# A third bank for the scores of the second attention, taken from the transposes

## The reference, cut to what matters

```python
q = _apply_rope(q, cos, sin)
k = _apply_rope(k, cos, sin)
k = jnp.repeat(k, groups, axis=2)
v = jnp.repeat(v, groups, axis=2)
scores = jnp.einsum('bqhd,bkhd->bhqk', q, k) * scale
scores = jnp.where(causal[None, None], scores, jnp.finfo(scores.dtype).min)
probs = jax.nn.softmax(scores, axis=-1)
attn = jnp.einsum('bhqk,bkhd->bqhd', probs, v).reshape(B, S, NH * HD)
```

## Time and profile before

| | us |
|---|---|
| median of 3 timed runs | 2964.31 (2962.42 to 2965.41) |
| the profiled execution's own time | 2973.27 |
| its span in the profile | 2971.6 |
| second attention: from the first transpose of a stack to the last score | 1585.9 to 2231.6 |
| PE / DVE / ACT / POOL busy over the whole span | 2476.5 / 1614.6 / 1474.1 / 903.1 |

### The profile page before, as it was taken

The page is one execution under the profiler, slowest core; times in us unless marked ns, Lnnn a source line. Parts: engine busy times, 40 slices in busy tenths (PEclk is TensorE's granted clock), DMA queues, the critical chain, the costliest instruction groups (busy, mean ns, idle before and its releaser), DMA issues. The chain is left out here.

```text
span 2971.6 us, 56781 instructions
## 1 busy us (share of the span) xinstructions
PE 2476.5 (83%) x12274; PEld 1400.6 (47%) x12275; DVE 1614.6 (54%) x4317; ACT 1474.1 (50%) x3174; POOL 903.1 (30%) x1721
## 2 busy tenths in 40 slices
PE   4999999999999999998366888898886508999980
PEld 3555565555655566555232333333324504666650
DVE  6666645666366655663586777777743301222227
ACT  3666645666366645563384766667763202222222
POOL 0344433444244434445031222222220171122210
PEclk7999999999999999998786999999989559999995
DMA  2000100001010110111233110111106422111114
GB/s 95 19 23 25 40 23 18 25 26 40 14 26 25 32 31 18 27 26 25 64 159 97 27 29 25 32 31 31 32 16 188 182 101 93 46 46 44 46 41 170
DMA packets 152514, 152.85 MB, mean 51 GB/s; under 512 B 66944, under 2 KB 122240, under 8 KB 150656
## 3 DMA queue, kind: packets, MB, share of 16 engines
q1 hardware_dynamic: 143680, 128.79, 14.3%
q0 software_dynamic: 6528, 17.87, 1.7%
q10 hardware_dynamic: 2112, 4.19, 0.4%
HBM read 87.80 MB, written 47.52 MB: 46 GB/s over the span
## 5 line engine op out<-in xcount | busy, mean ns | idle before, releaser
L1191 ACT ACTIVATE b_P<-b_SC 128x512 f32<-128x512 f32 (+3 forms) x768 | 347.2, 490 | 197.9 <-PE b_SC L1289 184.2
L296 POOL TENSOR_TENSOR a_A<-a_A,a_P 128x512 f32<-128x512 f32 (+3 forms) x320 | 321.4, 1004 | 304.4 <-PE a_O L600 291.8
L448 ACT ACTIVATE a_P<-a_SC 128x512 f32<-128x512 f32 (+3 forms) x640 | 293.4, 469 | 229.8 <-PE a_SC L583 189.8
L506 DVE CUSTOM_DVE_ANT_0 a_MX<-a_MX,a_causal 128x128 f32<-128x128 f32 (+3 forms) x512 | 250.0, 501 | 203.4 <-PE a_MX L649 191.6
L1238 DVE CUSTOM_DVE_ANT_0 b_MX<-b_MX,b_causal 128x128 f32<-128x128 f32 (+3 forms) x512 | 250.9, 500 | 146.4 <-PE b_MX L1333 127.0
L582 PE MATMUL a_SC<-a_QR,a_KR 128*128 128x512 f32 (+3 forms) x768 | 320.3, 421 | 7.0 <-DMA a_QS<-a_minusT 2.9
L649 PE MATMUL a_MX<-a_KR,a_QR 128*128 128x512 f32 (+3 forms) x768 | 290.2, 387 | 14.1 <-DVE a_peak L506 10.8
L1132 POOL TENSOR_SCALAR_AFFINE_SELECT b_P<-b_P 128x128 f32<-128x128 f32 x512 | 148.0, 294 | 503.6 <-ACT b_P L1191 495.8
L1289 PE MATMUL b_SC<-b_Q,b_K 98*128 98x512 bf16 (+3 forms) x768 | 254.5, 341 | 44.7 <-ACT b_P L1191 35.1
L1333 PE MATMUL b_MX<-b_K,b_Q 96*128 96x512 bf16 (+3 forms) x768 | 254.8, 343 | 16.0 <-ACT b_Q L1201 10.0
L583 PE MATMUL a_SC<-a_QS,a_KS 65*128 65x512 f32 (+3 forms) x768 | 266.4, 351 | 0.0
(11 more groups left out here) (243 smaller groups left out, 4145.4 us busy)
## 6 DMA issues: line engine op xcount, KB each, us to landing
a_inv<-inv_rows SPq DMA_DIRECT2D x128, 128.0 KB, 3.0
stack_rows<-p_stk SPq DMA_DIRECT2D x32, 480.0 KB, 2.6
a_W<-in_w_pair SPq DMA_DIRECT2D x34, 384.0 KB, 3.5
b_stk<-stack_rows SPq DMA_DIRECT2D x136, 96.0 KB, 2.0
e_G<-sorted_rows SPq DMA_DIRECT2D x74, 128.5 KB, 2.1
sorted_rows<-r_zeros SPq DMA_DIRECT2D x6, 1542.0 KB, 8.2
W<-in_w SPq DMA_DIRECT2D x8, 1024.0 KB, 11.8
n_x<-in_x SPq DMA_DIRECT2D x4, 1024.0 KB, 9.5
```

Of the source, the lines that this page charges most:

```text
L296: eng.tensor_tensor(acc[h][c][:, a:], acc[h][c][:, a:], buffer(n, h)[:, a:], ALU.add).then_inc(added[h], 1)
L448: act.activation(buffer(n, h)[:, a:], SC[h][:, a:], ACT.Exp, scale=DH1 ** -0.5).then_inc(s["exp_done"], 1)
L506: dve.tensor_tensor_reduce(MX[c % MAX_BANKS1][:, 0:w], MX[c % MAX_BANKS1][:, 0:w], causal[:, BANK - w:], 1.0, 3 * NEG, ALU.add, ALU.max, p ...
L1191: act.activation(probs[k % RING2][:, a:], SC[k % SCORE_BANKS][:, a:], ACT.Exp, scale=DH2 ** -0.5).then_inc(s["exp_done"], 1)
```

## The change

`TR` is gone as a bank of its own and becomes a view on the three `MX` banks; `SC` has three banks. The five stacks and 48 maxima of a step form one list, `SHARED`, in the order in which PE issues them, and take the three banks in turn. One semaphore per bank, `bank_used[b]`, replaces `max_used` and `stack_copied`: ACT raises it after it has copied a stack out of bank b, DVE after it has reduced a maximum there. A user of a bank waits for all earlier uses of that bank.

```diff
-SCORE_BANKS, MAX_BANKS = 2, 3
+SCORE_BANKS, MAX_BANKS = 3, 3
+SHARED = [x for k in range(NU2) for x in [("stack", n) for n, at in enumerate(STACK_SLOTS) if at == k]
+          + [("max", u) for u in MAX_AT.get(k, ())] + [("late", u) for u in MAX_AT.get(k + NU2, ())]]
+SHARED_BANK = {x: m % MAX_BANKS for m, x in enumerate(SHARED)}
+SHARED_USES = [sum(SHARED_BANK[x] == b for x in SHARED) for b in range(MAX_BANKS)]
+LATE_USES = [sum(SHARED_BANK[x] == b and x[0] == "late" for x in SHARED) for b in range(MAX_BANKS)]
+def used_so_far(n1, n2, x):
+    bank = SHARED_BANK[x]
+    mine = [y[0] for y in SHARED[:SHARED.index(x)] if SHARED_BANK[y] == bank]
+    if n2 is None:
+        return LATE_USES[bank] + len(mine) - mine.count("late")
+    if n1 is None:
+        return (n2 + 1) * SHARED_USES[bank] + mine.count("late")
+    return n1 * SHARED_USES[bank] + len(mine)
...
-        TR = ps("b_TR", [P, BANK])[0:STACK, :].bitcast(BF16)
+        TR = [m[0:STACK, :].bitcast(BF16) for m in MX]
+        bank_used = [sem(f"b_bank_used{i}") for i in range(MAX_BANKS)]
...
+                        bank = SHARED_BANK["stack", n]
-                            act.activation(K[p][0:STACK, :], TR, ACT.Copy).then_inc(s["stack_copied"], 1)
+                            act.activation(K[p][0:STACK, :], TR[bank], ACT.Copy).then_inc(bank_used[bank], 1)
...
-                    dve.tensor_reduce(peak[:, h, i, ch:ch + 1], MX[u % MAX_BANKS][:, 0:w], AX.X, ALU.max).then_inc(s["max_used"], 1)
+                    dve.tensor_reduce(peak[:, h, i, ch:ch + 1], MX[bank][:, 0:w], AX.X, ALU.max).then_inc(bank_used[bank], 1)
...
-                        dve.wait_ge(s["max_used"], n * NU2 + u + 1 + MAX_BANKS)
+                        at = SHARED.index(x)
+                        for y in SHARED[at - MAX_BANKS + 1:at + 1]:
+                            dve.wait_ge(bank_used[SHARED_BANK[y]], used_so_far(n1, n2, y) + 1)
...
+            def bank_free(n1, n2, x):
+                v = used_so_far(n1, n2, x)
+                if not isinstance(v, int) or v > 0:
+                    pe.wait_ge(bank_used[SHARED_BANK[x]], v)
...
-            def stack(n1, p, n):
+            def stack(n1, n2, p, n):
+                bank_free(n1, n2, ("stack", n))
...
-                if (i, ch) == MAXU[0]:
-                    stacked(n, h + 2)
-                pe.wait_ge(s["max_used"], n * NU2 + u + 1)
+                if x[0] == "max" and (i, ch) == MAXU[0]:
+                    for y in (("stack", 0), ("stack", h + 1)):
+                        pe.wait_ge(bank_used[SHARED_BANK[y]], used_so_far(n1, n2, y) + 1)
+                bank_free(n1, n2, x)
```

More of the change, by code:

```diff
@@ L1196, in step @@
                         n = STACK_SLOTS.index(k)
+                        bank = SHARED_BANK["stack", n]
                         act.wait_ge(s["stack_ready"], n1 * (GROUP + 1) + n + 1)
                         if n == 0:
-                            act.activation(K[p][0:STACK, :], TR, ACT.Copy).then_inc(s["stack_copied"], 1)
+                            act.activation(K[p][0:STACK, :], TR[bank], ACT.Copy).then_inc(bank_used[bank], 1)
                         else:
-                            act.activation(Q[p][0:STACK, :, n - 1, :], TR.rearrange("p (c s) -> p c s", c=2),
-                                           ACT.Copy).then_inc(s["stack_copied"], 1)
+                            act.activation(Q[p][0:STACK, :, n - 1, :], TR[bank].rearrange("p (c s) -> p c s", c=2),
+                                           ACT.Copy).then_inc(bank_used[bank], 1)
                     if n3 is not None and k == TAKE2[1]:
@@ L1214, in _ @@
             dve.wait_ge(s["consts"], 6)
-            dve.sem_inc(s["max_used"], MAX_BANKS)
+            for b in range(MAX_BANKS):
+                dve.sem_inc(bank_used[b], LATE_USES[b])
             dve.sem_inc(s["turn_copied"], 1)
@@ L1229, in rows_out, with reduce_max @@
                     inv[:, c, :, :].rearrange("p t (h a) -> p t h a", a=1).to_broadcast([P, 4, GROUP, DH2]), ALU.mult).then_inc(s["A2_done"], 1)
-            def reduce_max(n, u):
+            def reduce_max(n, u, n1, n2, x):
                 h, i, ch = MAX2[u]
                 w = min(BANK, (i + 1) * P - ch * BANK)
+                bank = SHARED_BANK[x]
                 dve.wait_ge(s["max_ready"], n * NU2 + u + 1)
@@ L1237, in reduce_max @@
                     dve.sem_inc(s["due"], 1)
[L1238 to L1239 removed]
+                    dve.tensor_tensor_reduce(MX[bank][:, 0:w], MX[bank][:, 0:w], causal[:, BANK - w:], 1.0, 3 * NEG,
+                                             ALU.add, ALU.max, peak[:, h, i, ch:ch + 1]).then_inc(bank_used[bank], 1)
                 else:
[L1241 removed]
+                    dve.tensor_reduce(peak[:, h, i, ch:ch + 1], MX[bank][:, 0:w], AX.X, ALU.max).then_inc(bank_used[bank], 1)
                 for c in range(2):
                     if u == HALF_MAX[c] - 1:
[L1244 removed]
+                        at = SHARED.index(x)
+                        for y in SHARED[at - MAX_BANKS + 1:at + 1]:
+                            dve.wait_ge(bank_used[SHARED_BANK[y]], used_so_far(n1, n2, y) + 1)
                         dve.tensor_reduce(minus[c][:, :, :], peak[:, :, 4 * c:4 * c + 4, :], AX.X, ALU.max,
@@ L1263, in step @@
                         if n1 is not None:
-                            reduce_max(n1, u)
+                            reduce_max(n1, u, n1, n2, ("max", u))
                     for u in MAX_AT.get(k + NU2, ()):
                         if n2 is not None:
-                            reduce_max(n2, u)
+                            reduce_max(n2, u, n1, n2, ("late", u))
                     for c, m in ((0, n1), (1, n2)):
@@ L1353, in step @@
                             pe.wait_ge(loaded[p], (n1 - p) * 72 + 144)
-                        stacked(n1, n)
-                        stack(n1, p, n)
+                        stack(n1, n2, p, n)
                     for u in MAX_AT[k]:
                         if n1 is not None:
-                            maximum(n1, p, u)
+                            maximum(n1, p, u, n1, n2, ("max", u))
                     for u in MAX_AT.get(k + NU2, ()):
                         if n2 is not None:
-                            maximum(n2, 1 - p, u)
+                            maximum(n2, 1 - p, u, n1, n2, ("late", u))
                     if n2 is not None and k == 0:
```

11 lines of the change are left out of this document (4 added, 7 removed).

## The result

The changed kernel took 2932.60 us (median, 2929.57 to 2934.54) against 2964.52 us; the ratio is 0.9892, with a 95% interval of 0.9875 to 0.9910. That is 32 us, or 1.1%, less. The forecast was 2902.8 us: the time is inside the stated range, but the gain is 52% of the 61.5 us forecast, and beyond the forecast's own range. Timed again beside later experiments the same kernel had a ratio of 0.9857 (0.9830 to 0.9884): 2925.35 us, 44 us less than the kernel before in that series (2969.85 us).

The account below looks back on a forecast made before the run. PE was taken to wait for score banks ACT had not emptied. Gains of 3.2 + 1.1 us a step, less a tenth 3.9, gave 58.5 us over fifteen steps, plus 3: 61.5 us less, 2902.8 us timed, range 2878 to 2940.

Parts of the forecast that it names:

- What bounds the kernel: Second attention: no engine is full; PE and ACT wait for each other because two score banks are too few.
- The size of the third bank's gain: Slots 16 to 47 of a step: from 24.58 to 21.4 us, a gain of 3.2 us.
- the walk: Slots 16 to 47 followed with measured distances and the new bank rules, PE and DVE leading by turns: 21.4 us.
- Slots 0 to 15: Gains of 0.4 us at score 3, 0.8 at score 11, 0.4 elsewhere: 1.6 us, before the sharing's cost.
- The shared banks: One ring for maxima and stacks costs 0.5 us a step: slot 4 0.2, stacks of slots 7, 11, 15 0.1 each.
- The last step: The step with scores alone, at a granted clock of 0.78 on average: 3 us saved.
- The sum: 4.3 us a step, less a tenth 3.9; fifteen steps 58.5 us, with the last step 61.5 us.
- Rival 1: DVE, as loaded as PE, takes over; a step saves 2.0 us instead of 3.9: 2932 us, chance 0.22.
- Rival 3: The shared ring in slots 0 to 15 holds PE; 3 us more a step, 3009 us, chance 0.05.
- Rival 4: Waits for ACT turn into equally long waits for DVE; no change, 2964 us, chance 0.03.
- The signs: Profile after: steps 34 to 35.5 us, `b_P` waits below 60, DVE waits 40 or more, ACT idle about 0.3.
- The sign for rival 3: Transposes or slot 4's maximum waiting over 1 us would show the shared ring holding PE.

Follow-up runs that it names:

- e3: The changed kernel with DVE's reductions of the second attention reading only the first half of each piece of the maxima; 2888.89 us, ratio 0.9744.
- e4: The kernel before the change with DVE's reductions reading only the first half of each piece of the maxima; 2959.62 us, ratio 0.9982.
- e1: The changed kernel with two score banks as before, stacks and maxima sharing three, one bank unused; 2972.31 us, ratio 1.0025.
- e7: The changed kernel with the first query stack turned in slot 3 instead of slot 2 and DVE's wait narrowed; 2930.52 us, ratio 0.9874.
- e9: The changed kernel with ACT copying the key stack before the first exponential of a step instead of after it; 2923.61 us, ratio 0.9854.
- e2: The changed kernel with two score banks and four banks shared by stacks and maxima, DVE's wait narrowed; 2960.64 us, ratio 0.9982.
- e5: The changed kernel with an unread 192-column memset on DVE after every fourth maximum; 2942.57 us, ratio 0.9918.
- e10: The changed kernel with only output unit 7 (slots 37 and 39) issued in two halves; 2918.79 us, ratio 0.9841.
- e6: The changed kernel with the six output units of 384 or 512 columns that don't open an accumulation issued in halves; 2944.45 us, ratio 0.9911.

## Why the prediction was right or wrong

**What bounds the kernel.** Right. PE's waits for exponentials in front of scores were the largest, and the third bank took two thirds of them away (209 to 71 us).

**The size of the third bank's gain.** Wrong, and this is the step that failed: "the walk gives 21.4 us" for slots 16 to 47, a gain of 3.2. Measured is 22.9, a gain of 1.6. The walk is not written out, so which of its slots went wrong cannot be read from it; two of its inputs can be compared with the traces. The first is the way through a bank of the maxima: the prediction puts a product of 0.39, a reduction of 0.70 and a read of 0.14 in a row, 1.23 us, already a little more than the 1.17 that PE needs from the first maximum to the fourth. The trace shows 1.39 us after an output unit, 0.57 of it before the reduction starts, so with three banks the fourth maximum waits. Shorter reductions (e3) take 2.0 us off slots 16 to 47 of the changed kernel, and in the kernel before (e4) 0.3, all of that in slots 44 to 47. That is the second: the walk had PE leading "at the step's end", where PE already waited for DVE in the kernel before. The prediction had checked this ring for the scores (T + 1.12 against T + 1.20) and never for the maxima, which stand in the same four slots and go through a slower engine.

**Slots 0 to 15.** A gain of 1.6 us before the sharing's cost was forecast, measured is 0.49 us: in even steps only slots 8 to 11 gained (3.98 to 3.49 between e1 and the changed kernel), where the prediction had score 11 delay the next stack; in odd steps slots 0 to 3 gained 0.24 besides. The 0.4 us at score 3 did not come, because the key copy ends at the same time (slot 2 above, e7); only an earlier copy moves it (e9).

**The shared banks.** The sum was right (0.5 forecast, 0.36 measured in even steps and 0.12 in odd ones; 7 us in all, of which 1.6 before the first score, a stretch that the prediction left out), the place partly: slot 4's wait for the copy cost nothing, slots 7 and 11 nothing, slot 15 all of it.

**The last step.** Forecast 3 us. At whole clock it took 29.8 us from its first to its last score in e2, with two score banks, and 25.2 us in e7, with three: 4.5 us. The profiled execution of the kernel before took 35.3 us there, at a granted clock of 0.78 on average, and that of the changed kernel 26.7 us at 0.94, so some 4 of these 8.6 us go with the clock:

```profile
2163.00:2194.00 31.00, 26.92 (x175) 8.31 (x174) 8.96 (x26) 21.94 (x55) 10.22 (x36) 0.94 0.01 1
```

**The sum.** 1.77 us in even steps, 2.27 in odd ones, in all 31.3 us over the fifteen steps of the profiled executions, of which 3.4 us are two steps of the kernel before with a lowered clock (40.6 and 40.8 us). The 27.9 us left are 1.9 a step, where the prediction had 3.9. With the last step's 4.5 us, less the 1.5 us that the stretch before the first score got longer, they give 31 us. The timed runs gave 32 us, and 44 us in the later series, so the close agreement with the first is in part luck. The tenth taken off for what a walk misses was far too little.

**The rivals.** Rival 1 had the time (2932), the saving of a step (2.0 us against 1.9) and the direction of its mechanism, DVE taking over. It put it down to DVE being as loaded as PE. That holds in slots 4 to 11, 24 to 27 and 36 to 39 (e5); after the other output units DVE idles first and the way through three banks is what is late. It had a chance of 0.22 and deserved more than the forecast. Rival 3 is refuted by e1: 7 us and not 117. Rival 4 happened to a good part: 138 us less of waiting for exponentials came with 60 us more for reductions (23 to 83) and 36 us more for ACT's copies of stacks (25 to 61), counted over PE's loads and products.

**The signs.** The waits for `b_P` fell to 71 us and not below 60, the steps came down to 36.7 us and not to 34 to 35.5, and ACT's idle time after the output unit of slots 32 to 35 is 0.59 us and not 0.3. These three point to the smaller gain. The waits in front of maxima for DVE rose to more than 40 us as forecast. The sign for rival 3 also showed, since the transposes of slot 2 wait up to 2.0 us for the key stack's copy, but it was badly chosen: that wait costs nothing (e7).

## What to carry to other kernels

When one of two rings that are served in turn gets another buffer, work out for the other ring as well how long a buffer takes to come round, from the product's start to the end of its reader, start-up included, with the engine empty as it is after a long burst. Look also for stretches in which that other reader already holds things up: there the new buffer gives nothing. The gain ends at whichever ring comes round later. Distances between the first instructions of small groups, as medians over steps, locate 0.3 us, where five timed executions left an interval of 7 us to either side (e10). They are to be taken over steps with the same granted clock: the last step seemed to gain 8.6 us, and 4.5 of them stay at whole clock.

## What the runs showed of the hardware

The granted clock of TensorE did not simply follow how much PE waited. In the changed kernel it stayed at 1.00 from 1656 to 2163 us, with PE busy for 90% of the time; in e6, with PE busy for 92% (33.18 of 36 us) between the dips, it fell to 0.84 on average over the stretch with the next step, and six of its fifteen steps took 2.3 or 5.5 us more. In the profiled execution, the slowest of the six, this makes the fifteen steps 20 us longer (569.8 against 550.2). The other five have no trace, but their mean granted clock over the whole program is 0.918 to 0.923, where the changed kernel's executions had 0.924 to 0.927, so the dips probably explain the 12 us of the timed runs, which the undisturbed steps do not show.

Behind the first step, every dip to 1.2 GHz in these fifteen steps began 2.1 to 4.2 us after the first score of a step that starts the loop's body: two in the kernel before, one each in e1, e2 and e3, five in e4, six in e6, and none in the other traces. Ahead of the dip PE is busy for less than half of the time: 1.04 us of the 2.7 from 1724.8 to 1727.5 in e6, and the clock is 0.50 from 1727.5 to 1741.2. But the changed kernel has the same place (1.48 us of the 2.7 from 1729.0 to 1731.7) and kept its clock. What decides between the two was not found.

A way from the start of a 512-column product to the start of its reader takes 0.52 us on ACT and 0.57 us on DVE when they are idle, on a product written as 0.39 us long.
